# Two edits in a four-layer transformer kernel: the top-k attention's input tiles are normalised by ScalarE, and the routing ranks are computed in expert-major order

## The reference, cut to what matters

```python
def _layernorm(x, axis=-1, eps=1e-05):
    return (x - mean(x)) / sqrt(var(x) + eps)

# third sub-layer, per batch of 256 tokens and 64 keys
q = query @ Wq.T + bq
scores = einsum('btd,bsd->bts', q, k) * scale
vals, idx = top_k(scores, 32)            # all other scores become -inf
attn = softmax(scores)
x = x + (attn @ v) @ Wo.T + bo

# fourth sub-layer, cap = 320
probs = softmax(x_norm @ Wg)             # 4096 tokens, 16 experts
top1_val, top1_idx = probs.max(-1), probs.argmax(-1)
masked = where(top1_idx[None, :] == arange(16)[:, None], top1_val[None, :], -inf)
vals, idx = top_k(masked, cap)           # the cap best tokens of each expert
y = x_norm, with the rows idx replaced by gelu(xe @ W1 + b1) @ W2 + b2
```

## Time and profile before

| | |
|---|---|
| median of 3 runs | 1411.47 us (1409.69 to 1411.76) |
| the profiled execution | 1411.86 us |
| its span in the trace | 1410.0 us |
| busy in the span | PE 1073.4 us, PEld 792.0, DVE 905.2, ACT 554.4, POOL 423.5 |
| top-k attention stage | from 446 to 561 us of the span |
| routing stage | from 561 to 713 us |
| expert stage | from 713 to 772 us |

### The profile page before, as it was taken

The page is one execution under the profiler, slowest core; times in us unless marked ns, Lnnn a source line. Parts: engine busy times, 40 slices in busy tenths (PEclk is TensorE's granted clock), DMA queues, the critical chain, the costliest instruction groups (busy, mean ns, idle before and its releaser), DMA issues. The chain is left out here.

```text
span 1410.0 us, 21638 instructions
## 1 busy us (share of the span) xinstructions
PE 1073.4 (76%) x6380; PEld 792.0 (56%) x6382; DVE 905.2 (64%) x3040; ACT 554.4 (39%) x1111; POOL 423.5 (30%) x463
## 2 busy tenths in 40 slices
PE   4788879999995765675478278857999999568842
PEld 1655669899993443632456155535567767445621
DVE  7777755656654888599822677756444445547768
ACT  2476434444443222232023256531334445446531
POOL 1344100000100111061262844401771457324311
PEclk9799969999997555555579569976999999869975
DMA  8344010000002300204032343200337751044202
GB/s 266 92 124 109 7 30 1 1 2 0 1 1 89 91 0 14 84 0 120 13 97 72 88 122 101 72 2 10 96 120 208 216 165 51 13 127 123 72 3 60
DMA packets 108320, 101.05 MB, mean 72 GB/s; under 512 B 10864, under 2 KB 88048, under 8 KB 107824
## 3 DMA queue, kind: packets, MB, share of 16 engines
q1 hardware_dynamic: 76464, 74.22, 18.5%
q0 software_dynamic: 6400, 12.92, 3.5%
q10 hardware_dynamic: 25344, 12.59, 3.1%
HBM read 62.13 MB, written 37.75 MB: 71 GB/s over the span
## 5 line engine op out<-in xcount | busy, mean ns | idle before, releaser
L858 DVE TENSOR_REDUCE mha_nm<-mha_pS 128x16 f32<-128x1024 f32 x96 | 117.2, 1221 | 25.0 <-PE mha_pS L620 24.8
L798 POOL TENSOR_TENSOR mha_ks<-KS,w_ctx 104x1024 fp32r<-104x1024 f32 (+1 forms) x48 | 90.8, 1893 | 94.7 <-POOLq L100 51.5
L1451 ACT ACTIVATE ffn_hid<-ffn_pH,w_ffn 128x512 f32<-128x512 f32 x128 | 85.5, 688 | 55.2 <-PE ffn_pH L1374 54.5
L741 ACT ACTIVATE XH<-mha_pST 128x1024 f32<-128x1024 f32 x96 | 97.8, 1018 | 10.5 <-PE mha_pST L641 10.4
L620 PE MATMUL mha_pS<-mha_ks,mha_qs 96*128 96x256 f32 (+1 forms) x384 | 79.7, 334 | 26.5 <-DVE mha_nm L858 20.0
L1387 PEld LDWEIGHTS ffn_pE<-W2R,ffn_hid 128*128 128x128 f32 x768 | 94.6, 194 | 4.4 <-issue 0.2
L1563 DVE SCALAR_TENSOR_TENSOR ffn_acc<-ffn_pE,ffn_wt,ffn_acc 128x128 f32<-128x128 f32 x192 | 54.0, 345 | 66.7 <-PE ffn_pE L1387 66.7
L1387 PE MATMUL ffn_pE<-W2R,ffn_hid 128*128 128x128 f32 x768 | 95.2, 278 | 0.0
L620 PEld LDWEIGHTS mha_pS<-mha_ks,mha_qs 96*128 96x128 f32 (+1 forms) x384 | 58.8, 212 | 42.0 <-issue 20.5
L2500 POOL DMA_INDIRECT leaf_rows<-XH,tree_place x64 | 63.2, 987 | 57.5 <-DVE tree_place L2580 38.3
L1479 POOL TENSOR_TENSOR X<-X,ffn_xh 128x512 f32<-128x512 f32 (+1 forms) x8 | 10.3, 1284 | 210.9 <-DVE ffn_xh L1509 210.9
(11 more groups left out here) (525 smaller groups left out, 2852.9 us busy)
## 6 DMA issues: line engine op xcount, KB each, us to landing
mha_qs<-queries SPq DMA_DIRECT2D x72, 256.0 KB, 4.0
tree_leaf<-in_leaves_dram SPq DMA_DIRECT2D x96, 96.5 KB
queries<-mha_qh SPq DMA_DIRECT2D x24, 256.0 KB, 2.1
queries<-mha_ql SPq DMA_DIRECT2D x24, 256.0 KB, 2.5
leaf_rows<-top_none SPq DMA_DIRECT2D x12, 512.0 KB, 6.7
tree_xs<-leaf_rows ACTq DMA_DIRECT2D x24, 256.0 KB, 3.2
leaf_results<-tree_ys ACTq DMA_DIRECT2D x24, 256.0 KB
EW<-in_L_W_dram SPq DMA_DIRECT2D x32, 128.0 KB, 2.6
```

Of the source, the lines that this page charges most:

```text
L741: act.activation(PT[b % PB][:, CU * i:CU * i + CU, :], pST[:], ACT.Exp, scale=SC).then_inc(s["P"], 1)
L798: pool.tensor_tensor(ks[b % KB][0:K1, :, :, :], kb, hb, ALU.mult).then_inc(s["k"], 1)
L858: dve.tensor_reduce(nm[:, t, :], pS[:], AX.X, ALU.max, negate=True).then_inc(s["nm"], 1)
L1451: act.activation(hid[p % 2][:, c, :], pH[c][:], ACT.Gelu, bias=b).then_inc(s["h"], 1)
```

## The change

In the attention, `normalise` moves from VectorE to ScalarE. It becomes an activation, `X * RS + NB`, with `NB = -mean * RS` made once by VectorE for all tokens. ScalarE does batches 0 and 1 ahead of the slots, batch 2 after the first two evacuations, and batch b+3 at the end of slot b, so one slot earlier than VectorE had it. ScalarE's loop covers slots 4 to 11 instead of 4 to 13. In the routing, `ca` and `kp` are used as they lie, `[P, N1, T]`, and `mv`, `oh`, the ranks and the bases are brought to that order by views; results of the f32 steps (`ranked`) lie expert-major too, and the two sums over experts read across.

```diff
@@ -991,16 +991,16 @@
                     pipeline(True)
 
 
-def batch_slots(eng, fn, lag):
+def batch_slots(eng, fn, lag, last=1):
 
     fn(0, 0)
     fn(1, 1)
     fn(2, 0)
     fn(3, 1)
-    with eng.Fori(2, B // 2 - 1) as i:
+    with eng.Fori(2, B // 2 - last) as i:
         fn(2 * i, 0)
         fn(2 * i + 1, 1)
-    for b in range(B - 2, B + lag):
+    for b in range(B - 2 * last, B + lag):
         fn(b, b % 2)
 
 
@@ -1061,13 +1061,14 @@
         pk = two("pk", [P, TB, P])
         PT = two("PT", [P, S])
         m8 = two("m8", [P, TB, TOP // R8, R8])
+        NB = st.sb("NB", [P, T])
         nm, sm, rc = two("nm", [P, TB]), two("sm", [P, TB]), two("rc", [P, TB])
         bn, mv = st.sb("bn", [P, TB, 6]), st.sb("mv", [P, TB, 2])
         pQ = st.ps("pQ", [P, 512])
         pS = [st.ps(f"pS{u}", [P, 512]) for u in range(2)]
         pT = st.ps("pT", [P, 512])
         pY = st.ps("pY", [P, 512])
-        names = "xh bo xTp xT qp q S sc top nm P pk PTp PT Y X bn own zero tick none".split()
+        names = "xh bo xTp xT qp q S sc top nm P pk PTp PT Y X bn own zero tick none nb".split()
         s = {n: st.sem(n) for n in names}
         none = st.sb("none", [P, P])
         rs_act, rs_dve = token_scales(core, st, MV[:, :, 1], RS[:], "a")
@@ -1120,6 +1121,13 @@
 
         @blk.scalar
         def _(act):
+            def normalise(b, u):
+                need(act, s["xTp"], b - 1)
+                for j in range(TB):
+                    t = TB * b + j
+                    ins = act.activation(xh[u][:, j, :], X[:, t, :], ACT.Identity, bias=NB[:, bass.ds(t, 1)], scale=RS[:, bass.ds(t, 1)])
+                ins.then_inc(s["xh"], 1)
+
             def x_evac(b, u):
                 need(act, s["xTp"], b + 1)
                 need(act, s["qp"], b - 1)
@@ -1144,12 +1152,18 @@
                 if live(b + 2):
                     x_evac(b + 2, u)
                     q_evac(b + 2, u)
+                if live(b + 3):
+                    normalise(b + 3, 1 - u)
 
             rs_act(act)
+            act.wait_ge(s["nb"], 1)
+            normalise(0, 0)
+            normalise(1, 1)
             for b in range(2):
                 x_evac(b, b)
                 q_evac(b, b)
-            batch_slots(act, slot, 2)
+            normalise(2, 0)
+            batch_slots(act, slot, 2, last=2)
 
         @blk.sync
         def _(sp):
@@ -1174,15 +1188,6 @@
         @blk.vector
         def _(dve):
             OWN = TB * 2 * (TOP // R8)
-
-            def normalise(b, u, tiles=range(TB)):
-                if 0 in tiles:
-                    need(dve, s["xTp"], b - 1)
-                for j in tiles:
-                    t = TB * b + j
-                    ins = dve.tensor_scalar(xh[u][:, j, :], X[:, t, :], MV[:, t, 0:1], RS[:, bass.ds(t, 1)], ALU.subtract, ALU.mult)
-                if TB - 1 in tiles:
-                    ins.then_inc(s["xh"], 1)
 
             def scaled(b, u):
                 need(dve, s["S"], b + 1)
@@ -1254,8 +1259,6 @@
                         best8(b, u, r)
                     if live(b - 2) and r < 2:
                         final(b - 2, u, 2 * r + 1)
-                    if live(b + 2) and r >= 2:
-                        normalise(b + 2, u, [r - 2])
                     if live(b):
                         mark8(b, u, r)
                 if live(b):
@@ -1264,8 +1267,7 @@
             for u in range(2):
                 dve.memset(pk[u][:, :, SK:P], 0.0).then_inc(s["zero"], 1)
             rs_dve(dve)
-            normalise(0, 0)
-            normalise(1, 1)
+            dve.scalar_tensor_tensor(NB[:], MV[:, :, 0], -1.0, RS[:], ALU.mult, ALU.mult).then_inc(s["nb"], 1)
             batch_slots(dve, slot, 2)
 
 
@@ -1663,7 +1665,7 @@
         xT = [st.sb(f"xT{u}", [P, GT * P]) for u in range(2)]
         chosen = st.sb("chosen", [P, 4 * T * N1])
         ex, oh, mv = (chosen[:, T * N1 * n:T * N1 * n + T * N1].rearrange("p (t e) -> p t e", e=N1) for n in range(3))
-        ca, kp = (st.sb(n, [P, N1, T], BF16)[:].rearrange("p e t -> p t e") for n in ("ca", "kp"))
+        ca, kp = (st.sb(n, [P, N1, T], BF16)[:] for n in ("ca", "kp"))
         upto, resume = (st.sb(n, [P, N1, T], BF16) for n in ("upto", "resume"))
         below, one16 = st.sb("below", [P, P], BF16), st.sb("one16", [P, P], BF16)
         WC = NCH * P
@@ -1704,6 +1706,9 @@
 
         blk = st.block()
         SH = [P, T, N1]
+        by_expert = lambda a: a.rearrange("p t e -> p e t")
+        EH_T = [P, N1, T]
+        over_tiles = lambda a: a.unsqueeze(2).to_broadcast(EH_T)
         bt = lambda a: a.unsqueeze(2).to_broadcast(SH)
         be = lambda a: a.unsqueeze(1).to_broadcast(SH)
 
@@ -1765,7 +1770,7 @@
             for n in range(2):
                 src = (ca, kp)[n]
                 pe.wait_ge(s["eqr"], n + 1)
-                pe.matmul(pP[:], below[:], src.rearrange("p t e -> p (e t)"), start=True, stop=False)
+                pe.matmul(pP[:], below[:], src.rearrange("p e t -> p (e t)"), start=True, stop=False)
                 pe.wait_ge(s["ca"], n + 1)
                 pe.matmul(pP[:], one16[:], upto[:].rearrange("p e t -> p (e t)"), start=False, stop=True).then_inc(s["prf"], 1)
             pe.wait_ge(s["lo"], HALVES)
@@ -1900,31 +1905,32 @@
             low(BITS + 3)
             dve.wait_ge(s["rowsp"], 1)
             link(dve.tensor_copy(rows[:], pR[:, 0:2 * N1]))
-            link(dve.tensor_tensor(ca, mv, be(rows[:, 0:N1]), ALU.is_equal))
+            link(dve.tensor_tensor(ca, by_expert(mv), over_tiles(rows[:, 0:N1]), ALU.is_equal))
             dve.wait_ge(s["bw"], 1)
             dve.wait_ge(s["res"], 2)
-            dve.tensor_tensor(ca, ca, oh, ALU.mult).then_inc(s["eqr"], 1)
+            dve.tensor_tensor(ca, ca, by_expert(oh), ALU.mult).then_inc(s["eqr"], 1)
             dve.wait_ge(s["eqr"], 1)
 
             def tiles_up_to(src):
 
                 dve.tensor_tensor_scan(upto[:].rearrange("p e t -> p (e t)"), resume[:].rearrange("p e t -> p (e t)"),
-                                       src.rearrange("p t e -> p (e t)"), 0.0, ALU.mult, ALU.add).then_inc(s["ca"], 1)
+                                       src.rearrange("p e t -> p (e t)"), 0.0, ALU.mult, ALU.add).then_inc(s["ca"], 1)
 
             tiles_up_to(ca)
-            link(dve.tensor_tensor(kp, mv, be(rows[:, 0:N1]), ALU.is_gt))
+            link(dve.tensor_tensor(kp, by_expert(mv), over_tiles(rows[:, 0:N1]), ALU.is_gt))
             dve.wait_ge(s["prf"], 1)
-            P3 = pP[:].rearrange("p (e t) -> p t e", e=N1)
-            link(dve.tensor_tensor(ex, P3, be(rows[:, N1:2 * N1]), ALU.is_lt))
-            link(dve.tensor_tensor(ex, ex, ca, ALU.mult))
-            dve.tensor_tensor(kp, kp, ex, ALU.add).then_inc(s["eqr"], 1)
+            P3 = pP[:].rearrange("p (e t) -> p e t", e=N1)
+            ranked = chosen[:, 0:T * N1].rearrange("p (e t) -> p e t", e=N1)
+            link(dve.tensor_tensor(ranked, P3, over_tiles(rows[:, N1:2 * N1]), ALU.is_lt))
+            link(dve.tensor_tensor(ranked, ranked, ca, ALU.mult))
+            dve.tensor_tensor(kp, kp, ranked, ALU.add).then_inc(s["eqr"], 1)
             dve.wait_ge(s["eqr"], 2)
             tiles_up_to(kp)
-            link(dve.tensor_reduce(sm[:], kp, AX.X, ALU.add))
+            link(dve.tensor_reduce(sm[:], kp.rearrange("p e t -> p t e"), AX.X, ALU.add))
             dve.wait_ge(s["prf"], 2)
-            link(dve.tensor_tensor(ex, P3, be(w("base")), ALU.add))
-            link(dve.tensor_tensor(ex, ex, kp, ALU.mult))
-            link(dve.tensor_reduce(mx[:], ex, AX.X, ALU.add))
+            link(dve.tensor_tensor(ranked, P3, over_tiles(w("base")), ALU.add))
+            link(dve.tensor_tensor(ranked, ranked, kp, ALU.mult))
+            link(dve.tensor_reduce(mx[:], ranked.rearrange("p e t -> p t e"), AX.X, ALU.add))
 
             link(dve.tensor_scalar(sm[:], sm[:], -float(2 * N1 * CAP), float(2 * N1 * CAP), ALU.mult, ALU.add))
             link(dve.tensor_tensor(slot[:], sm[:], mx[:], ALU.add))
```

## The result

The changed kernel takes **1397.57 us** (median of 4 runs, 1396.6 to 1400.4). The kernel before took 1411.62 beside it (4 runs, 1409.69 to 1414.37). The ratio is 0.9908, with a 95% interval of 0.9889 to 0.9927: 13.0 us less. I had forecast 1403.9 with a range down to 1399.5. The profiled execution took 1396.60, with a span of 1394.7.

What follows compares the result with a forecast made beforehand. VectorE was taken to bound the attention and routing stages. From the median 1411.47, 6.0 us off routing and 1.6 off attention (1.8 + 0.3 - 0.5) gave 1403.9 us, range 1399.5 to 1409.0.

Steps and rivals of the forecast that it cites:

- three across-reads: Routing: L1903, L1906 and L1915 read f32 in 64-byte steps after the change, 1.04 us each instead of about 2.38.
- 0.61 of TensorE beside the mark: Routing: L1915 at 1.04 still covers TensorE's matmul of the scan's result; if not, at most 0.61 us comes back.
- Rival (a): Routing: a strided read is as dear as a strided write, gain only 2.0 us, 1407.9 in all; chance 0.08.
- Rival (e): Routing: the change doesn't reach the end, since something other than `token` holds the gathers, 1409.9; chance 0.04.
- gaps from best8 to mark8: Attention, third and fourth rounds: without normalisations a loop slot gains 0.10 + 0.08, ten of them 1.8 us.
- the 2.3: Attention: GpSimd's bias add beside `keep` (L1216) costs VectorE 2.3 us in all in the kernel before.
- the price of what the moved add brings: Attention: the bias add, now following ScalarE, drifts against VectorE and holds up its operations, 2 us in all.
- Rival (b): Attention: the normalisations come off in full, 9.8 us instead of 1.8, giving 1395.9; chance 0.05.
- rival (c): Attention: the bias add locks with L1216 or L1244 in every slot, 7.9 lost instead of 0.3 won, 1412.1; chance 0.07.
- Rival (d): Attention: ScalarE becomes the bound, 8.9 us lost instead of 1.8 won, giving 1414.6; chance 0.04.
- nothing else stands between: Routing: only the first gather follows VectorE's chain, so a microsecond out of the chain is one off the total.
- A little of what stage timing may do: Range: an allowance, given no size, for effects on the stages behind, taken in with rival (a).

Runs made afterwards that it cites:

- e_route: Kernel before with only the routing half of the change: 1403.43 us (9 runs), ratio 0.9943 to before.
- e_top: Kernel before with only the attention half of the change: 1403.48 us (12 runs), ratio 0.9963 to before.
- e_pad: Changed kernel with the rank addition in routing done thirteen times instead of once: 1406.7 us (10 runs), ratio 0.9983 to before.
- e_held: Kernel before with GpSimd's bias add, from batch 2 on, also waiting for the slot's `keep`: 1405.98 us (10 runs), ratio 0.9969 to before.
- e_probe: Kernel before plus a stage of its own ahead of the last one, with 21 VectorE additions of one stride each: 1441.4 us (one run).

## Why the prediction was right, and where it failed

**Routing, forecast 6.0, measured 6.35: right.** The three across-reads were taken at 1.04 and were 0.99 to 1.02; the sum by the new rows is 9.51 - 3.70, plus 0.69, less 0.34, 6.16. `e_route` alone gave 6.17 in this stage; the other 0.2 came with the attention half (`e_top`: 151.37). The 0.61 of TensorE beside the mark stayed covered. Rival (a), the read as dear as the write, would have shown 2.38 in L1908. Rival (e) would have shown a gather that doesn't follow: it starts 133.4 us into the stage before and 127.1 after, and in `e_pad` the whole stage follows.

**Attention, forecast 1.6, measured 2.21: the mechanism right, one term mis-sized.** By the starts of the slots: slots 4 to 14 take 64.27 instead of 66.45 us (6.43 each, forecast 6.4), the first four 0.45 less, the tail 0.07 less, the head 0.49 more (forecast 0.5). The gaps from best8 to mark8 gave 1.8 as foreseen, and `e_held` confirmed the 2.3. With 0.5 lost in the head, a gain of 2.21 leaves 1.4 us for the term that failed, the price of what the moved add brings, taken at 2.0 from a drift even over the slot. Three operations were hit (L1249 by 0.35 and 0.10, L1211 by 0.38), 0.8 in all, then none: from 501 on the adds lie beside operations that aren't held up. Another 0.2 is a wait of `keep` for ScalarE's exponentials in slot 0, so ScalarE's new work was not quite free; 0.4 in short steps were not followed. Rival (b), normalisations off in full, asked for 9.8, and rival (c) for a hit in every slot. Rival (d) didn't happen: ScalarE did two tiles in 0.87 us, and behind the first slot VectorE waited for the scores just once, 0.4 us, at a turn of the loop where other turns have the same gap.

**The sum: it had no term for the stages further on.** The step "nothing else stands between" was right for its stage, and I took it as the whole effect. That is the step that failed: effects behind the edited stages stood at nothing. The edit changed the length of VectorE's program, and with it the entry of the tree stage, where VectorE is no longer 2.1 us late and the first matmul comes 1.7 us earlier. And it changed who is first at the entry of the last attention stage, where the first matmul comes 0.8 us earlier. Without these 2.5 us the median would have been near 1400, inside the range. No row of the attention or routing shows them. They stood in the trace of before, though. The wait of VectorE ahead of the tree stage names VectorE's own sequencer (5.27 us), where those at the other stage entries name TensorE's. And L962, which the earlier trace rows quotes for being held up, takes 1.90 us at the second place. That after would be rid of both could not be read from it: as to the forecast, this part of the gain is luck.

**The range: too narrow below.** It allowed 4.4 us, of which the attention and routing bounds took 3.1. The 6.3 us between forecast and median are the 2.5 above, the 1.0 by which the edited stages gave more than forecast, 1.7 not placed, and 1.1 by which the sum started too high: from a median of 3 runs, 1411.47, where the mean of all 79 runs of before is 1410.35. So the median fell 1.9 below the range. "A little of what stage timing may do" was no number; the traces show several us from trace to trace in stages with the same program.

## What to carry to other kernels

Cost an operation that is moved out of a wait by the gap that remains, not by its busy time, and look at what else its release triggers: here 32 normalisations of 0.35 us were worth 1.8, and the add that they released cost 2.3. When bf16 data must be transposed between two VectorE steps, let the reader do it and not the writer (1.0 against 2.4 us here). After a change, line up the traces behind it as well. An engine that is late at a barrier with nothing to wait for can owe it to its program's place; here a dozen free instructions moved it. And look at each stage entry for two operations that start within some hundredths of a microsecond of each other, one of which can hold up the other: an edit elsewhere can turn their order.

## What the runs showed of the hardware

- A VectorE addition of 128x512 that writes bf16 with 16 bytes or more from one element to the next takes 2.30 to 2.44 us, one that writes or reads f32, or reads bf16, with such steps 1.02 to 1.08, and without a stride 0.69 (`e_probe`). The strided operand in PSUM in before (L1918) costs nothing: 0.69.
- At one stage entry VectorE passed the barrier 2.1 to 2.4 us late, and shifting its program by 12 instructions took that away.
- VectorE's L962 takes 0.17 us when it starts 37 ns ahead of a GpSimd operation of 1.89, and 1.90 when it starts 27 ns behind it.
- VectorE's four-element copy takes 0.15 us, and 0.50 beside a GpSimd add of 0.72; the sum that reads PSUM beside the same add isn't longer.
